# Pacing a GpSimd gather stream by TensorE's progress instead of by a memset after each gather

## The reference

```python
e = jnp.stack([tbl_0[ids[:, 0]], ..., tbl_31[ids[:, 31]]], axis=1)   # 2048 x 32 x 64
gram = jnp.einsum('bnd,bmd->bnm', e, e)
rows, cols = jnp.triu_indices(32, k=1)
z = gram[:, rows, cols]                                              # 2048 x 496
h = jnp.concatenate([z, dense_ctx], axis=1)                          # 2048 x 512
h = jnp.maximum(h @ W_top1 + b_top1, 0.0)                            # 512 x 512
h = jnp.maximum(h @ W_top2 + b_top2, 0.0)                            # 512 x 256
y = h @ W_top3                                                       # 256 x 1
```

## Time and profile before

| | |
|---|---|
| Median of 3 runs | 508.75 us (504.62 to 510.11) |
| The profiled execution | 506.08 us, of it a span of 504.3 us from the first to the last instruction |
| TensorE matmuls busy | 423.6 us, 84% |
| GpSimd busy | 417.8 us, 83% |
| VectorE busy | 297.8 us, 59% |
| ScalarE busy | 114.6 us, 23% |
| Granted TensorE clock, mean | 0.929 of 2.4 GHz |
| DMA | 29.58 MB, mean 59 GB/s |

### The profile page before, as it was taken

One profiled execution on the slowest core, in us unless ns is written; L12 is line 12 of the kernel. 1 busy time (PEld: TensorE's weight loads), 2 busy tenths in 40 slices (PEclk: granted clock), 3 DMA queues, 4 the chain that ended last, 5 costly groups with the idle time before them and its releaser, 6 DMA issues.

```text
span 504.3 us, 10183 instructions
## 1 busy us (share of the span) xinstructions
PE 423.6 (84%) x4080; PEld 382.6 (76%) x4080; DVE 297.8 (59%) x361; ACT 114.6 (23%) x206; POOL 417.8 (83%) x538
## 2 busy tenths in 40 slices
PE   5398589995299989979799969988999959993887
PEld 5387479984298879869698869868897949883765
DVE  2599779794094589448483749339753948250400
ACT  2244312131011321123012311132103300230311
POOL 7999999998898899888998989889998899885010
PEclk9699799997599999999799979999899979996999
DMA  4444631012301122112301123112311231111010
GB/s 109 140 141 149 205 137 22 17 33 51 102 15 23 25 60 98 22 26 61 102 17 24 40 57 88 22 27 56 102 21 21 54 84 44 24 35 44 1 43 2
DMA packets 22070, 29.58 MB, mean 59 GB/s; under 512 B 9910, under 2 KB 14198, under 8 KB 20896
## 3 DMA queue, kind: packets, MB, share of 16 engines
q1 hardware_dynamic: 12980, 18.96, 10.9%
q0 software_dynamic: 8640, 8.86, 10.7%
q10 hardware_dynamic: 404, 1.09, 0.5%
HBM read 24.61 MB, written 0.07 MB: 49 GB/s over the span
## 4 chain that ended last, share of the span: by engine, by line
POOL 82%; issue 9%; PE 4%; DMA 2%; SPq 1%; DVE 1%; ACT 1%; DVEq 0%; ACTq 0%
POOL rows L253 59%; POOL pause L260 23%; PE mlp_ps L328 1%; PE gram_ps L316 1%; SPq L192 1%; PE mlp_ps L338 1%; DVE folded L530 1%; ACT folded L441 0%; DMA rows<-tbl,index 0%; PE gram_ps L352 0%; SPq L219 0%; DMA index<-ids 0%; DMA pairs<-dense 0%; DMA pairs<-folded 0%; PE turn_ps L289 0%
## 5 line engine op out<-in xcount | busy, mean ns | idle before, releaser
L253 POOL DMA_INDIRECT rows<-tbl,index x264 | 299.4, 1134 | 45.9 <-issue 43.3
L303 PE MATMUL turn_ps<-split_sb,onehot 125*128 125x192 bf16 x2192 | 210.4, 256 | 19.9 <-DVE split_sb L544 17.3
L303 PEld LDWEIGHTS turn_ps<-split_sb,onehot 125*128 125x128 bf16 x2192 | 192.9, 102 | 27.8 <-DVE split_sb L544 18.7
L495 DVE TENSOR_TENSOR onehot<-place,codes_wide 125x2048 bf16<-125x2048 f16 (+1 forms) x127 | 168.1, 1325 | 7.3 <-DMA place<-ids_scratch 7.3
L260 POOL MEMSET pause<- 128x384 f32 x264 | 115.7, 438 | 0.2
L503 DVE TENSOR_REDUCE rows<-turn_ps 128x128 f32<-128x384 f32 x124 | 68.8, 556 | 70.8 <-PE turn_ps L303 68.1
L530 DVE COPY_PREDICATED folded<-second_sb,gram_ps 128x512 f32<-128x512 int32 x64 | 46.6, 729 | 81.8 <-ACT folded L441 81.7
L316 PE MATMUL gram_ps<-emb_t 64*128 64x128 f32 x1024 | 74.0, 286 | 3.3 <-DVE folded L530 3.3
L316 PEld LDWEIGHTS gram_ps<-emb_t 64*128 64x128 f32 x1024 | 62.7, 190 | 17.7 <-issue 13.3
L289 PE MATMUL mlp_ps<-ident_sb,rows 128*128 128x128 f32 x240 | 39.1, 288 | 40.8 <-DMA rows<-tbl,index 34.5
L441 ACT COPY folded<-gram_ps 128x512 f32<-128x512 f32 x64 | 37.5, 586 | 152.0 <-PE gram_ps L316 152.0
(11 more groups left out here) (28 smaller groups left out, 75.8 us busy)
## 6 DMA issues: line engine op xcount, KB each, us to landing
place<-ids_scratch SPq DMA_DIRECT2D x8, 1000.0 KB
rows<-tbl,index POOLq DMA_INDIRECT x264, 2.7
pairs<-folded SPq DMA_DIRECT2D x122, 32.0 KB
emb_t<-tbl SPq DMA_DIRECT2D x8, 250.0 KB
folded<-tbl SPq DMA_DIRECT2D x5, 312.5 KB
w_sb<-w SPq DMA_DIRECT2D x1, 1024.0 KB
place<-ids_scratch ACTq DMA_DIRECT2D x1, 750.0 KB
rows<-tbl SPq DMA_DIRECT2D x2, 312.5 KB
```

The lines of the kernel that those rows point to most:

```text
L253: nc.gpsimd.indirect_dma_start(rows[:, s % 2, slot, t, :], None, tables[f][:, :], bass.IndirectOffsetOnAxis(index[:, s, t, f:f + 1], 0),). ...
L303: last = nc.tensor.matmul(turn_ps[:, u % 2].rearrange("p k b -> p (k b)")[:, t * PARTS * DIM:(t + 1) * PARTS * DIM], onehot[:, u % RING, c ...
L495: nc.vector.tensor_tensor(onehot[:, u % RING, 0:SPAN[u], :], place[:, parity, u, :].unsqueeze(1).to_broadcast([TP, SPAN[u], SUPER]), codes ...
```

## The change

Super tiles 0 and 1 are gathered as before, each gather with its memset. From super tile 2 on there is no memset; in its place stands, before each gather, a wait on one of TensorE's own semaphores. `pe_marks(s)` lists what TensorE raises in the step of s, in order, each with a cost: 8 or 10 for a look-up (its span), 3 for a turn group, 7 for a gram batch, 21 for half of layer 1 and for layer 2. Their running sum, divided by the total, gives the share of the step that is done at each mark. The n-th of the 32 gathers of super tile s waits for the last mark at or before the place s - 1 - 0.25 + n/32, counted in steps: the first for a mark three quarters through step s-2, the last for one at 0.72 of step s-1. The wait for `turned_drained` stays.

```diff
+PACED_BY_PE, LEAD = 2, 0.25
+TURN_COST, GRAM_COST, LAYER_COST = 3, 7, 21
...
+        def pe_marks(s):
+
+            marks = []
+            for g in range(GROUPS):
+                marks += [(lookup_ready, FIRST_UNITS + UNITS * s + u + 1, SPAN[u]) for u in TURN_UNITS[g]]
+                marks.append((turned, GROUPS * s + g + 1, TURN_COST))
+            for k in range(GRAM_BATCHES):
+                marks += [(lookup_ready, FIRST_UNITS + UNITS * s + u + 1, SPAN[u]) for u in GRAM_UNITS[k]]
+                if s and k in LAYER1_BEFORE:
+                    marks.append((layer1_ready, 2 * (s - 1) + LAYER1_BEFORE.index(k) + 1, LAYER_COST))
+                if s and k == LAYER2_BEFORE:
+                    marks.append((layer2_ready, s, LAYER_COST))
+                marks.append((gram_ready, GRAM_BATCHES * s + k + 1, GRAM_COST))
+            cost = sum(mark[2] for mark in marks)
+            done = np.cumsum([mark[2] for mark in marks]) / cost
+            return [(semaphore, value, end) for (semaphore, value, _), end in zip(marks, done)]
+
+        def mark_at(place):
+
+            s = int(place)
+            passed = [(semaphore, value) for semaphore, value, end in pe_marks(s) if end <= place - s]
+            return passed[-1] if passed else pe_marks(s - 1)[-1][:2]
...
                     for t in range(TILES):
+                        if s >= PACED_BY_PE:
+                            nth = TILES * (slot - begin) + t
+                            pool.wait_ge(*mark_at(s - 1 - LEAD + nth / (TILES * (FIELDS - begin))))
                         nc.gpsimd.indirect_dma_start(
                             rows[:, s % 2, slot, t, :], None, tables[f][:, :],
                             bass.IndirectOffsetOnAxis(index[:, s, t, f:f + 1], 0),
                         ).then_inc(rows_landed[s % 2][slot // GROUP_F], 16)
-                        before = next(pauses)
-                        if before:
-                            pool.wait_ge(paused, before)
-                        nc.gpsimd.memset(pause[:], 0.0).then_inc(paused, 1)
+                        if s < PACED_BY_PE:
+                            before = next(pauses)
+                            if before:
+                                pool.wait_ge(paused, before)
+                            nc.gpsimd.memset(pause[:], 0.0).then_inc(paused, 1)
```

## The result

The change made the kernel slower: 524.31 us median (523.71 to 527.79) against 506.69 (503.44 to 510.11), ratio 1.0361 with a 95% interval of 1.0269 to 1.0453. Two later measurements gave 1.0284 (1.0203 to 1.0366) and, from two runs only, 1.031 (1.011 to 1.050). I had forecast 471 us.

What follows compares the result with a forecast made beforehand. GpSimd was taken as the slower stream, 55.6 us a super tile against TensorE's 48.3. Removing TensorE's waits saves 37.6: 506.08 - 37.6 = 468.5, plus 2.67 for the median, 471 us; own range 464 to 476, chance 0.64.

Steps and rivals of the forecast that it cites:

- So one step of TensorE without waits is 226.14 - 172.82 - 2.43 - 2.61 = 48.3 us: TensorE's step 2, less its row wait and loop jump, gives 48.3 us a step, against GpSimd's 55.6.
- rival 4: TensorE's clock falls to its lower level under load without waits; a step grows 34 us, two steps give 539; chance 0.07.
- What TensorE would save: Steps 2 to 7, if rows were always there: 2.4 + 13.8 + 11.2 + 7.7 + 2.5 = 37.6 us.
- 7.7 + 2.5: Step 7: the 7.74 us wait for rows, and half of the 4.98 us of TensorE work at clock 0.50 behind it.
- everything behind group 7 of the last step: End of step 7: a fixed chain of TensorE, copies and moves of `pairs`, claimed to stay, so no saving.
- GpSimd's pace: Undisturbed gathers without memset: 0.95 us plus 0.16 before each, 1.12 from start to start; 48.4 us a super tile.
- rival 1: GpSimd's dispatch after a wait is felt: gathers 1.41 us apart instead of 1.12; 491, half effect 476 to 480; chance 0.17.
- The rule of one gather for each one-hot: Look-up stage: a gather ends 0.83 us behind the running one-hot, so one per one-hot; removing the memset gives nothing there.
- Rival 2: Gathers keep VectorE out: a one-hot loses about 0.9 us at three places a step, 13.5 us, so 484; chance 0.06.
- 23.7 us of distance: Marks bind only if GpSimd is over 0.49 x 48.3 = 23.7 us early; it is 7 to 8, so none holds a gather.

Runs made afterwards that it cites:

- e14: Kernel before with plain copies of 128 table rows, each with a memset 640 wide, replacing gathers from super tile 2 on: 475.0 us.
- e13: The kernel before, unaltered, traced in a batch without stalls: 505.7 us.
- e16: Kernel before without memsets and without marks from super tile 2 on, in a batch without stalls: 478.8 us, ratio 0.9436.
- e18: Kernel before with plain copies of 128 table rows, each with a memset, replacing gathers from super tile 2 on, in a stalling batch: 475.7 us.
- e8: The changed kernel, but super tile 2 keeps its memsets and marks begin with super tile 3; batch without stalls: 483.5 us, ratio 0.9572.
- e12: Kernel before without memsets and marks from super tile 2 on, gathers there fetching only 64 rows, in a stalling batch: 639.8 us.
- e10: Kernel before without memsets and without marks from super tile 2 on, repeated in a second stalling batch: 626.5 us.
- e2: Kernel before without memsets and without marks from super tile 2 on, in the first, stalling batch: 647.0 us.
- e1: The changed kernel with all memsets kept beside the marks, in a stalling batch: 502.7 us, ratio 0.9918 to the kernel before.
- e5: Kernel before without memsets and marks from super tile 2 on, gathers there fetching only 64 rows, in a batch without stalls: 473.4 us.
- e4: Kernel before with the memset 128 wide instead of 384 from super tile 2 on, no marks, in a stalling batch: 619.8 us.

## Why the prediction was wrong

**The step that failed** is "So one step of TensorE without waits is 226.14 - 172.82 - 2.43 - 2.61 = 48.3 us", used as a price that would hold once gathers stood closer. I took it from a trace in which no two gathers ever stood under 1.55 apart, and asked only whether GpSimd could keep up, whether it would hold VectorE, and whether the transfers would land. That GpSimd's gathers could hold up TensorE's own matmuls and the signals between engines stood in no row, and I gave it no rival; rival 4 had the right sign, with the clock as its mechanism. The clock did fall, but behind the stalls (142 to 144 us above).

**What the runs showed in its place:** in the changed kernel two steps without a wait for rows take 110.0 us instead of 96.6, and the stretch before step 3 is 23.2 us longer than it was. Where nothing is held up the price was right. In e14, TensorE's timeline has

```profile
224.46 0.65 PE L293 MATMUL mlp_ps<-ident_sb,rows 128*128 128x128 f32 x4 [2.93 <-issue]
...
323.23 0.65 PE L293 MATMUL mlp_ps<-ident_sb,rows 128*128 128x128 f32 x4 [2.71 <-issue]
...
419.21 0.66 PE L293 MATMUL mlp_ps<-ident_sb,rows 128*128 128x128 f32 x4
```

so steps 3 and 4 take 323.23 - 2.71 - 224.46 = 96.1, and step 7 begins at 419.2, where I had 419.

**What TensorE would save.** The sum of 37.6 us came near. With plain copies, where rows are never late and nothing stalls, the span is 471.9 (e14) against 503.4 for the kernel before in the same batch (e13): 31.5. The missing 6 lie in step 7, for which I had 7.7 + 2.5 less than 57.6, that is 47.4, and which takes 52.7. Most of it is one wait that I had ruled out by "everything behind group 7 of the last step" staying. ScalarE and TensorE in e14's last step:

```profile
433.37 1.07 ACT L445 COPY folded<-gram_ps 128x512 f32<-128x512 f32 x2 [9.48 <-DMA pairs<-folded]
...
434.88 3.46 PE L320 MATMUL gram_ps<-emb_t 64*128 64x128 f32 x32 [4.60 <-DVE folded L534]
```

The first fold of step 7 may not overwrite `folded` before the moves of step 6 have read it. With group 7 no longer late, these moves are: 4.60 us, and slow clock behind it (32 matmuls in 3.46 us; 2.06 at full clock). A stall went, and what was late next was a transfer. I had asked that question of the marks and not of this step.

**GpSimd's pace.** I took 1.12 from start to start; in every trace with two full gathers in a row they stand 1.25 apart, with 0.30 before a gather that follows a gather instead of 0.17. This is nearly half of rival 1's 0.29, and it isn't the wait at marks: e16 has none and the same 0.30. In e16 two waits for rows are left after step 1.

```profile
287.04 0.78 PE L290 MATMUL mlp_ps<-ident_sb,rows 128*128 128x128 f32 x4 [2.37 <-DMA rows<-tbl,index]
...
436.73 0.66 PE L290 MATMUL turn_ps<-ident_sb,rows 128*128 128x128 f32 x4 [4.26 <-DMA rows<-tbl,index]
```

2.37 in step 4 and 4.26 in the last, so 478.8 and not 475. The rule of one gather for each one-hot held in e16: 1.76 apart in the turn groups, 1.87 and 2.48 behind.

**VectorE was not held.** One-hots took 1.22 and 1.48 to 1.49 at 1.25 spacing. Rival 2 falls. The rule beside it (the Trainium skill, "SBUF — State Buffer", the section on the two separate sides of SBUF) is borne out here only where the one-hot comes first, as the rows of before had said. I had also applied it too simply: the one-hot has two inputs from SBUF, and for such an operation the Trainium skill, in that section, limits the lock to a GpSimd operation that reads SBUF. The traces add which transfer is held. In e16 the 86 gathers that start under a one-hot end 0.81 to 0.83 us behind its end. In e18 the 67 plain copies that do take 0.54 us in the median, like the ones that don't, and stand 1.10 apart through the look-ups.

**The marks did bind**, against my 23.7 us of distance, because TensorE was late, not GpSimd early. In e8, where nothing stalls, no gather from super tile 3 on waits more than 0.31 us: there no mark holds one, as I had forecast.

**What stays open.** Which path the gathers crowd. The share of the DMA engines is no sign of it: 0.07 to 0.15 in the stalled windows 190 to 220 of e12, e10 and e2, 0.24 in the same window of e16. Why some batches stall and others don't. Whether an execution that isn't being recorded stalls at all: every run behind these medians has its span and clock on record, and all traces of the stalling batches lose events, so the recording itself is a rival for the cause that no run here tests. It would have to be more than the number of events, for e18 keeps 1,160 of them between 150 and 200 us and e16 838. Whether the kernel before loses events in such a batch; no trace of it was taken in one, only e1's. And what the change takes in a batch without stalls: it didn't run there. By e16 (478.8, without marks) and e8 (483.5) some 475 to 484 would be likely, an estimate, against my 471.

## What to carry to other kernels

A filler instruction can be doing work that no row shows: before taking it out, ask what has never happened in the trace because of it (here two gathers under 1.55 us apart), and price that separately. Which pace is best depends on the condition. In a stalling batch only the distance of 1.55 was harmless, and 1.44 already cost 56 us; where nothing stalls, catching up at 1.25 (478.8) beats a bound of 1.50 (499). None of the variants is shown to beat the kernel before in both kinds. And repeat a surprising run unaltered on another chip before building on it: two of my batches would have told opposite stories.

## What the runs showed of the hardware

All of this is from executions that were being recorded.

- Gathers of GpSimd 1.25 us apart brought TensorE down to one matmul in 2.8 us (e2) and delayed a signal between engines by 13 us (the changed kernel). It came in three of five batches and in the first measurement of the change; in the two others the same files (e16, e5, e8) ran without a stall.
- In a stalling batch (e1 to e4) the median grew by 56 us at 1.44 us, by 114 at 1.34 and by 141 at 1.25, and not at 1.55. The runs at 1.34 and 1.25 overlap (610 to 629, 619 to 660).
- It follows the number of gathers: 64 rows each instead of 128 stall as much (639.8, 626.5). Plain copies of the same bytes 1.10 apart, with a memset behind each, did not.
- The traces of the stalling batches lose semaphore events while gathers run, with or without a stall (e1 4,929 events of some 8,000), and not while plain copies run (e18).
- An indirect gather costs GpSimd 0.90 us for 64 rows and 0.95 for 128; 0.30 us lie between two of them, 0.17 behind a memset.
- A running one-hot holds an indirect gather until 0.81 to 0.83 us behind its end (e16); it does not hold a plain copy (0.54 us with it or without, e18).
